# Weighted sums of the index scores on GpSimd, and minima and top-k of VectorE one slot later

## What is computed

```python
q_i = (x @ idx_wq).reshape(B_, L_, N_IDX_HEAD, D_HEAD)      # 4 index heads of 64
k_i = x @ idx_wk
s_i = jax.nn.relu(jnp.einsum('bthd,bsd->bths', q_i, k_i))
I = jnp.einsum('bths,h->bts', s_i, idx_w)                   # the weighted sum over the 4 heads
I = jnp.where(local[None], jnp.inf, I)
I = jnp.where(causal[None], -jnp.inf, I)
_, idx = jax.lax.top_k(I, kk)                               # 96 keys of each query
```

## Time and profile before

| | |
|---|---|
| median of 3 runs | 690.98 us (687.41 to 692.0) |
| profiled execution, its own time | 683.81 us |
| its span, first to last instruction | 682.0 us |
| mean granted TensorE clock | 0.906 of 2.4 GHz |
| busy: PE / PEld / DVE | 578.3 / 441.2 / 479.7 us (85 / 65 / 70%) |
| busy: ACT / POOL | 362.2 / 268.4 us (53 / 39%) |
| steps 0 to 6 begin at | 39.6, 100.3, 163.2, 227.1, 297.7, 368.3, 446.6 us |
| chain that ended last: PE / DVE / POOL | 31 / 10 / 10% of the span |
| DVE groups L1723, L1726, L1728 of both sums, 8 batches | 28.1 us busy |

### The profile page before, as it was taken

The page is one execution under the profiler, slowest core; times in us unless marked ns, Lnnn a source line. Parts: engine busy times, 40 slices in busy tenths (PEclk is TensorE's granted clock), DMA queues, the critical chain, the costliest instruction groups (busy, mean ns, idle before and its releaser), DMA issues.

```text
span 682.0 us, 22130 instructions
## 1 busy us (share of the span) xinstructions
PE 578.3 (85%) x8149; PEld 441.2 (65%) x8149; DVE 479.7 (70%) x1746; ACT 362.2 (53%) x1253; POOL 268.4 (39%) x428
## 2 busy tenths in 40 slices
PE   5379977996898789989997788979996998789996
PEld 4255654664566456776786566757885677678886
DVE  1948848986986798569965896679767685434653
ACT  4344545563655446637764554566654444554352
POOL 1415812911570287014801698418403563104310
PEclk9657797898899769989998799799998897999999
DMA  5030163113013142463335143543362524686551
GB/s 166 13 110 17 23 194 122 22 33 111 13 23 112 27 134 54 149 198 98 108 111 160 44 145 84 162 150 110 98 198 79 176 76 111 199 236 197 178 164 42
DMA packets 58594, 75.85 MB, mean 111 GB/s; under 512 B 14256, under 2 KB 47480, under 8 KB 57336
## 3 DMA queue, kind: packets, MB, share of 16 engines
q1 hardware_dynamic: 56952, 71.30, 35.1%
q0 software_dynamic: 1536, 3.15, 1.6%
HBM read 58.92 MB, written 8.62 MB: 99 GB/s over the span
## 4 chain that ended last, share of the span: by engine, by line
PE 31%; DVE 10%; POOL 10%; issue 8%; ACT 6%; DMA 1%; SPq 0%; DVEq 0%; POOLq 0%; ACTq 0%
PE bW L1352 4%; PE bH L1287 3%; PE bR L1302 3%; PE bG L1075 3%; POOL gb L851 3%; PE bM L919 2%; ACT qV L1549 2%; PE bH L1338 2%; PE bG L1338 2%; PE bS L1094 2%; PE bM L1122 1%; PE bM L1117 1%; ACT ht L1581 1%; POOL sorted_tokens L863 1%; PE bC L1227 1%
## 5 line engine op out<-in xcount | busy, mean ns | idle before, releaser
L1495 ACT ACTIVATE pp<-pp,nmx 128x224 f32<-128x224 f32 x96 | 46.5, 485 | 98.3 <-DVE nmx L1813 98.2
L1820 DVE TENSOR_TENSOR gs<-bG,rank_t 96x512 f32<-96x512 f32 x96 | 65.4, 681 | 11.8 <-PE bG L1075 11.6
L809 POOL TENSOR_TENSOR r<-x,cst 128x256 f32<-128x256 f32 x8 | 5.8, 726 | 145.3 <-DVE x L1847 145.3
L1075 PE MATMUL bG<-oh,kspl 128*96 128x512 f32 x160 | 59.4, 454 | 0.0
L1801 DVE TENSOR_SCALAR ppn<-pp,rls 128x224 f32<-128x224 f32 (+1 forms) x128 | 48.8, 382 | 14.5 <-PE bM L919 0.5
L1581 ACT ACTIVATE ht<-bH,wt 128x128 f32<-128x128 f32 x156 | 44.7, 375 | 22.1 <-PE bH L1287 22.1
L1883 DVE TENSOR_TENSOR sm<-bC,cst 128x512 f32<-128x512 f32 x64 | 43.4, 679 | 15.2 <-PE bC L1227 15.0
L919 PE MATMUL bM<-cst,ppn 128*128 128x128 f32 (+1 forms) x224 | 51.1, 300 | 3.2 <-DVE ppn L1801 3.2
L1227 PE MATMUL bC<-qV,kS 128*128 128x512 f32 x64 | 34.6, 540 | 17.3 <-DVE sm L1883 11.8
L1507 ACT COPY pts<-bM 128x256 f32<-128x256 f32 x96 | 35.0, 365 | 25.8 <-PE bM L919 25.3
L1302 PE MATMUL bR<-wt,ht 128*128 128x128 f32 x264 | 40.0, 300 | 9.4 <-DVE taken L1963 9.3
(11 more groups left out here) (294 smaller groups left out, 1583.8 us busy)
## 6 DMA issues: line engine op xcount, KB each, us to landing
wt<-in_experts SPq DMA_DIRECT2D x61, 578.0 KB, 4.1
sidx<-far_slots SPq DMA_DIRECT2D x8, 1536.0 KB, 6.8
vstk<-gs SPq DMA_DIRECT2D x96, 64.0 KB
xs<-sorted_tokens SPq DMA_DIRECT2D x45, 64.0 KB, 3.9
expert_rows<-ot SPq DMA_DIRECT2D x45, 64.0 KB, 3.6
sorted_tokens<-acc SPq DMA_DIRECT2D x9, 256.0 KB, 2.9
cst<-shape_constants SPq DMA_DIRECT2D x1, 1595.5 KB, 6.4
xn<-in_x SPq DMA_DIRECT2D x8, 128.0 KB, 3.2
```

Source lines behind the costliest of these rows:

```text
L1075: last = MM(w[0:96, :], table, oh[:, pair % 2, kt, SLOTS * (tile % 2):SLOTS * (tile % 2) + SLOTS], start=(n == 0), stop=(n == len(products ...
L1495: AC(pp[:, s % 2, 0:w], bS[:, 0:w] if s < T0 else pp[:, s % 2, :], ACT.Exp, scale=1.0 if s < T0 else -1.0, bias=nmx[:, s % 2:s % 2 + 1], a ...
L1820: TT(gs[:, g % 2, :].rearrange("p (t j) -> p t j", j=FAR), bG[0:96, :].rearrange("p (t j) -> p t j", j=FAR), rank_t[:, :].rearrange("p (o ...
```

## The change

The weighted sums of batches 1 to 7 move from VectorE to GpSimd, at the same own slots 4 and 5. GpSimd has no fused form in the new code: a sum is 4 products (tensor_scalar by one pointer scalar) and 3 additions (tensor_tensor), with a wait of GpSimd on itself between a product and its addition, and one behind the last. The products of heads 1 to 3 go to `g1` and `g2`. The minimum with the table stays on VectorE, in own slot 6 for A and own slot 7 for B, ahead of the top-k there, and waits there for GpSimd's semaphore `a_sum`. All of top-k begins one own slot later (A from 6, B from 7) and its last instruction stands in own slot 12, ahead of the casts. Batch 0's sums stay on VectorE in own slots 4 and 5. `ra` is given free to ScalarE by the minima of the batch before (`a_cut`), which were also what it waited for before.

```diff
--- before.py
+++ after.py
@@ -377,7 +377,7 @@
         a_free = sig("a_free", 15, 2)
         own_aa = sig("own_aa", 6, 1)
         a_soft = sig("a_soft", 3, 1)
-        own_va = sig("own_va", 10, 1)
+        own_va, own_gw, a_sum, a_cut = sig("own_va", 0), sig("own_gw", 14), sig("a_sum", 2), sig("a_cut", 2, 1)
         own_vq, v_q = sig("own_vq", 8), sig("v_q", 1)
         top_a, top_b = sig("top_a", 11, 1), sig("top_b", 11, 1)
         a_slot = sig("a_slot", 2, 1)
@@ -730,8 +730,31 @@
             oc = Own(pool, own_gc)
             hv = lambda ap: ap.rearrange("p (h a d) -> p h a d", a=2, d=16)
 
+            ow = Own(pool, own_gw)
+
+            def weighted(raw, dst, n, one, two):
+
+                k = ow.did(nc.gpsimd.tensor_scalar(dst, raw[:, 0, :], idxw[0:n, 0:1], None, ALU.mult))
+                for h in range(1, NIH):
+                    part = (one, two)[h % 2]
+                    m = ow.did(nc.gpsimd.tensor_scalar(part, raw[:, h, :], idxw[0:n, h:h + 1], None, ALU.mult))
+                    ow.wait(m)
+                    k = ow.did(TT(dst, dst, part, ALU.add))
+                ow.wait(k)
+                pool.sem_inc(a_sum.sem, 1)
+
             def stage_a(s, i):
                 oa.batch(s, i.n)
+                if s < 0 and not i.first:
+                    ow.batch(s, i.n - 1)
+                if s == 4 and not i.first:
+                    pool.wait_ge(a_free.sem, a_free.at(i.n, 5))
+                    pool.wait_ge(top_a.sem, top_a.at(i.n - 1, 11))
+                    weighted(ra, sa[:, :], 128, g1[:, 0:128], g2[:, 0:128])
+                if s == 5 and not i.first:
+                    pool.wait_ge(a_free.sem, a_free.at(i.n, 7))
+                    pool.wait_ge(top_b.sem, top_b.at(i.n - 1, 11))
+                    weighted(rb, sbb[:, :], 64, g1[0:64, 0:192], g2[0:64, 0:192])
                 if s == 6:
 
                     pool.wait_ge(a_soft.sem, a_soft.at(i.n, 3))
@@ -1432,7 +1455,7 @@
                         full(3 + r)
                         if r == 0:
 
-                            act.wait_ge(own_va.sem, own_va.at(i.n, 0))
+                            act.wait_ge(a_cut.sem, a_cut.at(i.n, 0))
                         free(AC(ra[:, r::2, :], ring(3 + r)[:, 0:256].rearrange("p (c n) -> p c n", c=2), ACT.Relu))
                 if s == 4.5:
                     for r in range(2):
@@ -1621,7 +1644,7 @@
 
         @block.vector
         def _(dve):
-            for s_ in (own_va, g_top, r_ks, r_qs, top_a, top_b, a_slot, o_ready, g_out, s_max, s_rec, s_nrm, c_freeV, ln_st, own_vc,
+            for s_ in (a_cut, g_top, r_ks, r_qs, top_a, top_b, a_slot, o_ready, g_out, s_max, s_rec, s_nrm, c_freeV, ln_st, own_vc,
                        c_x1, c_x2, r_lg, r_m, r_place, own_vd, own_vf, f_st, ln_root):
                 dve.sem_inc(s_.sem, s_.per * s_.lead)
             TT, TS, STT = nc.vector.tensor_tensor, nc.vector.tensor_scalar, nc.vector.scalar_tensor_tensor
@@ -1725,13 +1748,13 @@
                     ov.wait(k)
                     k = ov.did(STT(dst, raw[:, h, :], idxw[0:n, h:h + 1], dst, ALU.mult, ALU.add))
                 ov.wait(k)
-                ov.did(TT(dst, dst, cut, ALU.min))
+                TT(dst, dst, cut, ALU.min).then_inc(a_cut.sem, 1)
 
             def top(i, k, sig_, s_, v, idx):
 
                 r, what = k // 3, k % 3
                 if k == 0:
-                    dve.wait_ge(own_va.sem, own_va.at(i.n, 5 if sig_ is top_a else 10))
+                    dve.wait_ge(a_cut.sem, a_cut.at(i.n, 1 if sig_ is top_a else 2))
                 else:
                     dve.wait_ge(sig_.sem, sig_.at(i.n, k))
                 settled()
@@ -1745,17 +1768,20 @@
                 ins.then_inc(sig_.sem, 1)
 
             def stage_a(s, i):
-                ov.batch(s, i.n)
-                if s == 4:
+                if s == 4 and i.first:
                     dve.wait_ge(a_free.sem, a_free.at(i.n, 5))
                     weighted(ra, sa[:, :], C("cut_a"), 128)
-                if s == 5:
+                if s == 5 and i.first:
                     dve.wait_ge(a_free.sem, a_free.at(i.n, 7))
                     weighted(rb, sbb[:, :], C("cut_b", 64), 64)
                 if s == 9 and not i.first:
                     top_keys(i)
+                if s in (6, 7) and not i.first:
+                    dve.wait_ge(a_sum.sem, a_sum.at(i.n - 1, s - 5))
+                    dst, cut = ((sa[:, :], C("cut_a")), (sbb[:, :], C("cut_b", 64)))[s - 6]
+                    TT(dst, dst, cut, ALU.min).then_inc(a_cut.sem, 1)
                 for d in range(2) if s == int(s) else ():
-                    ka_, kb_ = 2 * (s - 5) + d, 2 * (s - 6) + d
+                    ka_, kb_ = 2 * (s - 6) + d, 2 * (s - 7) + d
                     if 0 <= ka_ < 11:
                         top(i, ka_, top_a, sa[:, :], va, ia)
                     if 0 <= kb_ < 11:
@@ -2072,7 +2098,7 @@
                     TS(accd[d][:, r, :], accd[d][:, r, :], fmv[:, r, 0:1], fln[:, 5, r:r + 1], ALU.subtract, ALU.mult).then_inc(e_ln.sem, 1)
 
             program(stage_a, stage_b, stage_c, stage_d, tile_list, fetch, tile, collect, summed, means, normed, dense_first, dense_second, dense_end)
-            assert ov.k == own_va.per and oc.k == own_vc.per, (ov.k, oc.k)
+            assert oc.k == own_vc.per, oc.k
```

## The result

The changed kernel takes 707.93 us (median of 5 runs, 705.89 to 709.84), the kernel before 690.98; the ratio is 1.0278, with an interval of 1.0240 to 1.0316. It is slower by 17 us on the medians and by 19 on the ratio, where 10 were forecast. The profiled execution took 707.19 us, its span is 705.4, its granted TensorE clock 0.902 in the mean, against 0.906 before.

The account below looks back on a forecast made before the run. TensorE and ScalarE were taken to end slots 2 and 3 in ordinary steps, VectorE to be full in slots 8 to 10. 8.4 (steps 3 and 5) + 1.5 (top-k) = +9.9 us, on the 690.98 median 701; range 691 to 708.

Parts of the forecast that it names:

- dear product: Upper end of GpSimd's product price, 1.18 us at 192 columns, making B 6.8 us; the range reaches up over it.
- Relief in ordinary steps: Slots 2 and 3: sums leaving VectorE lie under TensorE and ScalarE; 0.26 us gain against 0.35 for minimum B, together 0.
- Rival 2: VectorE ends slots 2 and 3 after all, so relief is felt: -10 us, 681; chance 0.12.
- The price of B: Sum B on GpSimd: 4 products of 0.76, 3 additions of 0.60, 4 waits of 0.08, 5.2 us; ends 3.5 and 6.8.
- Rival 1: Cheap products: each costs a cast's 0.34 us, B 3.5, whole change +5.0 to +6.5, 696.0 to 697.5; chance 0.20.
- GpSimd in ordinary steps: Steps 0, 1, 2, 4, 6: B is done before minimum B is due in slot 5, no wait, cost 0.
- Steps 3 and 5: B behind 8 indirect DMAs delays slot 5's negated maximum by 4.9 and 3.5 us, 8.4 together.
- Rival 3: The delay of steps 3 and 5 is half made up by TensorE in slots 6 to 8: +4.2, 695.2; chance 0.12.
- Top-k one slot later: Slots 9 and 10 gain 0.7 and 0.34 us per step, felt only in steps 1 to 3: 0 to 3.1, taken 1.5.
- TensorE as the cover in tile steps: Where experts' tiles run, TensorE was to cover the later top-k's 1.0 us per step.
- Contention: GpSimd beside VectorE: they hold each other up, but B stretched to 178.2 still precedes slot 5 at 180.13; cost 0.

Follow-up runs that it names:

- kernel 3: The kernel before without the weighted sums of batches 1 to 7 (minimum of head 0 stays on VectorE), nothing shifted: 680.84 us, 0.9895 of before.
- experiment 7: The changed kernel with sum B formed ahead of the 8 indirect DMAs on GpSimd in steps 3 and 5: 701.74 us, 1.0187 of before.
- kernels 3 and 4: Both lack the sums of batches 1 to 7; the second also has minima and top-k one slot later: 688.4 us, 0.9997 of before.
- experiment 2: The kernel before with all sums kept on VectorE, only minima and top-k one slot later: 692.95 us, 1.0096 of before.
- experiment 6: The kernel before, with GpSimd also forming the sums of the five ordinary steps into unread spare buffers: 690.92 us beside 689.99, 1.0018.
- experiment 1: The changed kernel with the sums of steps 3 and 5 back on VectorE, top-k still shifted in all seven: 692.97 us, 1.0078 of before.

## Why the prediction was wrong

It had the direction and the mechanism in steps 3 and 5, and came out 7 us short on the medians. That the range reaches up to 708, where the median stands, is luck: it reaches there over a dear product (a B of 6.8 us), and the product came out as forecast.

- **Relief in ordinary steps, 0: right in sum, its bound not.** The prediction gave the mark of slot 3 in step 6 no more than 0.3 us; it came 1.2 earlier, and slot 2's 1.7. But stretches 3 and 4 gave it back: in kernel 3, without sums, 0.1 to 0.3 us is left at slot 4 in steps 0, 1, 2 and 4. Rival 2 has nothing for it. The 0.35 us for the minimum of B is what stretch 4 measured.
- **The price of B, 5.2 us: right.** It is 4.99 in steps 3 and 5, with 0.76 us a product, and 5.6 to 6.0 in the five others, stretched. Sum A was put at 3.4 us, at most 4.5; it takes 4.1 to 5.3, and nobody waits for it. Rival 1's 0.34 is out. The Trainium skill (GPSIMD Engine Reference, 4.1 Engine selection) puts one-input operations at roughly line rate; the trace does not agree: the undisturbed product of 64x192 takes 0.76 us, the cast of the same shape 0.343 after the change.
- **GpSimd in ordinary steps, 0: right**, no wait at either minimum there; in step 2 B ends 2.5 us before its minimum begins.
- **Steps 3 and 5, 8.4 us: near.** The mark of slot 5 is 5.5 and 4.3 us late, 9.8 in all, against 4.9 and 3.5. The part that was off is the start of the 8 DMAs: forecast 1.7 us sooner, it came 1.1 and 0.2 sooner, and their end 1.0 and 0.7. Rival 3 had TensorE make up half of it in slots 6 to 8; nothing is made up there (+7.2 and +6.9 by slot 10). In step 5, though, 3.4 us are made up at slot 12, in VectorE's old wait for GpSimd's sum, so that this step is 3.0 us late at slot 15. The forecast had seen the two delays of step 5 as one, and counted them once. What it did not see is that the 8 DMAs, B and the key tables are one list: experiment 7 removes the minimum's wait and meets the next.
- **Top-k one slot later, 0 to 3.1, taken 1.5: this step failed.** It measured 0.96% alone and 1.03% without sums, some 7 us. The load was counted rightly, 0.7 us in slot 9 and 0.34 in slot 10 of each step. What failed is the cover: the cost was taken as felt only in steps 1, 2 and 3, and half of it there, since TensorE was to cover it where tiles run, GpSimd's chain in step 5, and VectorE's light load in step 0. Between kernels 3 and 4 stretch 8 grows by 0.67 to 0.97 us in all seven steps, 5.3 us together, and the slots ahead of it did not just pass their load on (1.4 us in stretches 5 to 7). Slot 10's part came to 0.5 us in all. From slot 5 on there were 16 top-k instructions and are now 20, with the minimum of B: five times 0.35 = 1.7 us a step. The runs give 1.0 a step, so a part is hidden.
- **TensorE as the cover in tile steps: wrong in slot 9.** The prediction read it from the row of step 4 in the earlier trace rows. That row is stretch 9 and holds no top-k before the change; the three instructions of slot 9 stand in the stretch ahead of it. Before, and with the shift alone (experiment 2):

```profile
330.50:333.24 2.74, 2.74 (x41) 2.02 (x42) 2.63 (x11) 2.21 (x9) 2.53 (x7) 1.00 0.62 196
...
332.73:336.44 3.71, 3.71 (x100) 2.95 (x87) 3.33 (x14) 2.23 (x9) 3.36 (x9) 1.00 0.42 137
336.44:340.84 4.40, 4.40 (x74) 3.54 (x73) 4.29 (x13) 2.15 (x6) 3.32 (x4) 1.00 0.42 97
```

Stretch 8 grew by 0.97 us although TensorE is busy in all of it in both kernels: it took in 59 matmuls more, so busy in full said that there was work to do, and not that it had to be done there. Stretch 9 grew as well, from 3.86 to 4.40 us, but stretch 10 behind it fell from 3.17 to 2.42: for slot 10 the cover held. In the changed kernel itself stretch 9 of step 4 did not grow.

- **Contention, 0: near.** 0.18% by experiment 6, at most 0.47%. The Trainium skill (SBUF — State Buffer, "Who interferes with whom") says that VectorE and GpSimd exclude each other in such instructions; the rows agree in part, with a minimum of B that takes 525 ns in the mean, where 352 stood in the earlier trace rows and 0.34 to 0.47 us with the shift alone, yet all of it is worth about 1 us of the kernel.

The parts agree within their intervals, which are 0.3 to 0.45% wide on either side: 0.96% for the shift, less the little relief of the ordinary steps, and 0.18% for contention, against the 0.78% of experiment 1. The list steps have the rest, 1.98%, which is a quotient of two measured ratios and no sum of its own; the traces give it 13.8 us (experiment 1). That is more than the 9.8 at slot 5, since experiment 1 also gains at that mark, 1.1 and 0.6 us, and the marks run on. Left open is how much of the shift's cost is the top-k and how much the minimum of B, which no run moved alone, how much the granted clock has of the shift and of steps 3 and 5, and whether the free time of stretch 12 can be used.

## What to carry to other kernels

When work is moved by a slot, add up what enters and leaves each slot that an engine fills, and take none of it as covered because another engine is busy in full there: only a run in which the load changes says who ends the slot. Before reading free time off a row, look in the timeline whether the instructions in question stand before or behind the mark that the row starts at; the prediction and three of the experiments here were off by one slot. Before giving work to an idle engine, look for the one step where its list is long, since a sum of 5 us behind 8 DMAs cost more than all the relief; the part that stands ahead of them (sum A alone) gained 0.1 to 0.8%.

## What the runs showed of the hardware that was not expected

In steps 3 and 5 of the changed kernel the last six of GpSimd's 8 indirect DMAs occupy its list for 1.26 us each, 0.96 of work and 0.30 of issue, without waiting for data; all 8 take 10.5 and 10.2 us. The same product of 64x192 took 0.758 us in the median and up to 1.634. In experiment 6, with a mean of 0.98 over 15 such products that nobody waited for, the kernel gained or lost no time that could be told.
